# The second state-space unit prepared beside the first one's scan, and loads in another order

## The reference, cut to what matters

```
x = norm(x + state_space(x))     # Mamba-like: convolution, delta = softplus(..), scan over time with 256 x 16 states
x = norm(x + moe(x))             # 16 experts, top 2, and a shared expert
x = norm(x + lstm_attention(x))  # an LSTM of width 20 gives position weights over x
x = norm(x + 4 layers of moe(x)) # 4 experts of width 512, top 2
```

```
h = exp(d_t * A) * h + d_t * b_t * u_t;  y = sum_s(h * c_t)      # then y + D * x_d, times silu(z), projection
c = sigmoid(f) * c + sigmoid(i) * tanh(g);  h = sigmoid(o) * tanh(c)
```

## Time and profile before

| | |
|---|---|
| median of 3 runs | 3143.62 us (3141.18 to 3147.69) |
| the profiled execution, own time | 3143.73 us |
| its span | 3141.7 us |
| mean granted TensorE clock | 0.803 |
| instructions | 30770 |
| HBM read, written | 195.36 MB, 7.34 MB |

### The profile page before, as it was taken

The page is one execution under the profiler, slowest core; times in us unless marked ns, Lnnn a source line. Parts: engine busy times, 40 slices in busy tenths (PEclk is TensorE's granted clock), DMA queues, the critical chain, the costliest instruction groups (busy, mean ns, idle before and its releaser), DMA issues.

```text
span 3141.7 us, 30770 instructions
## 1 busy us (share of the span) xinstructions
PE 2537.0 (81%) x7208; PEld 1271.2 (40%) x7208; DVE 1943.4 (62%) x6569; ACT 1386.7 (44%) x4620; POOL 1062.8 (34%) x913
## 2 busy tenths in 40 slices
PE   4776884479996989789886998788978997889598
PEld 1122443244444444344444443444444444444344
DVE  4857587357775777567766677577766555444422
ACT  3232433435544555445544554445534444444233
POOL 4735257104542445235432455244422001100200
PEclk7587655659996899878996899789978996788699
DMA  3231332003321233113220332122311220111021
GB/s 108 68 84 54 89 99 72 25 13 100 101 66 28 80 96 90 42 46 101 78 71 27 92 97 75 25 73 84 92 33 46 65 64 21 34 64 58 10 81 57
DMA packets 111774, 204.70 MB, mean 65 GB/s; under 512 B 14799, under 2 KB 24422, under 8 KB 111592
## 3 DMA queue, kind: packets, MB, share of 16 engines
q1 hardware_dynamic: 111592, 202.75, 22.1%
HBM read 195.36 MB, written 7.34 MB: 65 GB/s over the span
## 4 chain that ended last, share of the span: by engine, by line
PE 41%; DVE 28%; ACT 14%; issue 7%; POOL 1%; DVEq 0%; POOLq 0%; ACTq 0%
PE p_hid L656 8%; DVE state L1197 7%; PE p_turn L905 7%; PE p_misc L666 4%; ACT cell_t L919 4%; DVE cell L935 3%; DVE add_c L932 3%; PE p_acc L666 3%; DVE weighed L1206 2%; DVE p_turn L929 2%; PE p_misc L354 2%; PE p_gate L465 2%; DVE hist L940 2%; PE p_turn L475 1%; ACT cand L916 1%
## 5 line engine op out<-in xcount | busy, mean ns | idle before, releaser
L905 PEld LDWEIGHTS p_turn<-hist,w_hh 22*128 22x128 f32 x2048 | 371.6, 225 | 1148.2 <-DVE hist L940 1013.9
L905 PE MATMUL p_turn<-hist,w_hh 22*128 22x4 f32 x2048 | 457.3, 291 | 420.2 <-DVE hist L940 402.2
L656 PE MATMUL p_hid<-xhat,w 128*128 128x512 f32 x1024 | 581.8, 652 | 1.1 <-ACT hid L714 0.7
L919 ACT ACTIVATE cell_t<-cell 20x4 f32<-20x4 f32 x1024 | 207.7, 203 | 701.7 <-DVE cell L935 701.7
L1135 POOL TENSOR_TENSOR drive<-du,rows 128x512 f32<-128x512 f32 x256 | 473.4, 1849 | 63.2 <-DVE state L1197 44.9
L929 DVE SCALAR_TENSOR_TENSOR p_turn<-p_turn,cell 20x4 f32<-20x4 f32 x1024 | 170.7, 167 | 500.8 <-ACT p_turn L915 478.9
L714 ACT ACTIVATE hid<-p_hid,b1f 128x512 f32<-128x512 f32 x512 | 351.6, 687 | 243.1 <-PE p_misc L666 151.1
L388 POOL TENSOR_TENSOR n_rstd<-n_var,minus_half 128x4 f32<-128x4 f32 x56 | 62.0, 1108 | 1098.3 <-DVE n_var L376 1098.3
L1197 DVE TENSOR_TENSOR_SCAN state<-decay,drive 128x512 f32<-128x512 f32 x256 | 398.1, 1555 | 25.2 <-POOL drive L1139 15.7
L1154 POOL TENSOR_TENSOR y<-y,weighed 128x512 f32<-128x512 f32 x192 | 242.4, 1262 | 450.5 <-DVE weighed L1206 449.9
L940 DVE SCALAR_TENSOR_TENSOR hist<-p_turn,cell_t 20x4 f32<-20x4 f32 x1024 | 162.7, 159 | 275.6 <-ACT cell_t L919 275.6
(11 more groups left out here) (204 smaller groups left out, 3161.5 us busy)
## 6 DMA issues: line engine op xcount, KB each, us to landing
rows<-rows_dram SPq DMA_DIRECT2D x128, 512.0 KB, 5.0
w<-w_dram SPq DMA_DIRECT2D x128, 256.0 KB, 2.7
w<-in_w2T SPq DMA_DIRECT2D x128, 256.0 KB, 2.7
comb_b<-comb_dram SPq DMA_DIRECT2D x64, 512.0 KB, 4.7
rows<-comb_dram SPq DMA_DIRECT2D x128, 128.0 KB, 2.9
w<-in_w1T SPq DMA_DIRECT2D x16, 256.0 KB, 2.8
w_dram<-w SPq DMA_DIRECT2D x16, 256.0 KB, 2.4
out_xT<-result SPq DMA_DIRECT2D x8, 256.0 KB, 2.5
```

What stands on the lines that cost most here:

```text
L656: nc.tensor.matmul(p_hid[:, v % 2, :], w1[:, v // FB, (v % FB) * P:(v % FB + 1) * P], xhat[:, :], start=True, stop=True).then_inc(g_h, 1)
L905: nc.tensor.matmul(gate_bank(i)[:, :, t:t + 1], w_hh[:, :], before, start=False, stop=False, skip_group_check=True).then_inc(gates_done, 1)
L919: nc.scalar.activation(cell_t[64:64 + PE_, :], cell[32:32 + PE_, :], ACT.Tanh, scale=0.5).then_inc(cell_tanh, 1)
```

## The change

Unit 1 gets storage of its own, in tiles that are not yet in use then, and PSUM banks of its own for its preparation. `first_units` writes the opening anew: unit 0's preparation, then the late loads (on SP), its soft part, its scan with the preparation and ten of the soft slots of unit 1 beside, the leaving of unit 0 with the rest of unit 1's soft part, the scan of unit 1, its leaving, and then unit 2 whole (preparation, soft part, scan, leaving) and the preparation of unit 3. `opening` runs this to the end of unit 0 and then 60 slots of it with layer 0 of chunk 0 beside. `first_period` starts the LSTM there; the rest of the unit schedule goes on beside it, layer 0 of chunk 1 once unit 1 has left, the fold once unit 2 is prepared. `EARLY` is 3, and `scan(u)` in `first_units` passes `True`, so unit 2 is an early unit as well. In a slot the LSTM comes first, then layer 0, the fold, and the units. `mamba_soft_pool` makes both skip terms first and the `kc` products after the drives of the unit before are done. The periods from 1 on keep their order.

```diff
+    as_bt = lambda t: t[:, :, :].rearrange("p j (b t) -> p j b t", b=B)
+    second = dict(xd=comb_b[:, 0:2, :], zs=comb_b[:, 2:4, :], delta=as_bt(xl), du=hid1[:, :, :], y=terms[:, :, :], inc=mw[:, :, :])
+    first = dict(xd=xd[:, :, :], zs=zs[:, :, :], delta=delta[:, :, :, :], du=du[:, :, :], y=y[:, :, :], inc=weighed[:, :, :])
+    of_unit = lambda u: second if u == 1 else first
...
+    def banks(u):
+        if u == 1:
+            return (p_gate[:, :], p_up[:, :]), p_turn[1][:, :], p_turn[0][:, :]
+        return (p_hid[:, 0, :], p_hid[:, 1, :]), p_acc1[:, :], p_misc1[:, :]
...
-        if u:
+        if u > 1:
             pe.wait_ge(ssm_taken, u)
-        if 0 < u <= EARLY:
+        if 1 < u <= EARLY:
             pe.wait_ge(gated, u * NB)
...
         nc.sync.wait_ge(ssm_stored, 16 * (u + 1))
-        for s_ in range(ROWS):
-            load_rows(u, s_)
+        if u != 1:
+            for s_ in range(ROWS):
+                load_rows(u, s_)
...
-    SOFT = 13
+    SOFT, SOFT_A = 14, 10
...
         for j in range(NB):
             pool.wait_ge(delta_done, u * NB + j + 1)
-            nc.gpsimd.tensor_tensor(kc[:, j, :, :], a_neg[:, j, :].rearrange("p (s o) -> p s o", o=1).to_broadcast([P, S, B]),
-                                    delta[:, j, :, 0:1].rearrange("p b o -> p o b").to_broadcast([P, S, B]),
-                                    ALU.mult).then_inc(kc_arg, 1)
-            nc.gpsimd.tensor_scalar(y[:, j, :], xd[:, j, :], d_par[:, j:j + 1], None, ALU.mult).then_inc(y_begun, 1)
+            nc.gpsimd.tensor_scalar(of_unit(u)['y'][:, j, :], of_unit(u)['xd'][:, j, :], d_par[:, j:j + 1], None, ALU.mult)\
+                .then_inc(y_begun, 1)
             yield
             if j == 0:
                 yield
+        if u:
+            pool.wait_ge(drive_done, u * NS)
...
-            if j == 1 and s_ + ROWS - 1 < S and s_:
-                load_rows(u, s_ + ROWS - 1)
+            n = s_ + ROWS - 1
+            if j == 1 and s_ and n < S:
+                load_rows(u, n)
+            if u == 0 and j == 1 and n >= S:
+                load_rows(1, n - S)
+            if u == 1 and k == 0:
+                load_rows(1, ROWS - 1)
...
-    EARLY = 2
+    EARLY = 3
...
+    L0_SLOTS = 60
+    FOLD_SLOTS = 3 * L * E1 + 14
...
+    def first_units(of, seen):
+        get = lambda what, n, u, *a: of[what](u, *a) if what in of else nothing(n)
+        pre = [get("pre", PRE, u) for u in range(EARLY + 1)]
+        soft = [get("soft", SOFT, u) for u in range(EARLY + 1)]
+
+        def scan(u, beside):
+            burst = of["decays"](u) if "decays" in of else nothing(NS)
+            g = get("scan", SCAN, u, True)
+            for k in range(SCAN + 1):
+                for _ in range(6 if k == 0 else 1 if k % 2 == 0 else 0):
+                    next(burst, None)
+                next(g, None)
+                if k:
+                    next(beside, None)
+                yield
...
+        def before(u):
+            yield from run(pre[u], PRE + 1)
+            yield from run(soft[u], SOFT_A)
+
+        yield from run(pre[0], PRE + 1)
+        if "late" in of:
+            of["late"]()
+        yield from run(soft[0], SOFT + 1)
+        yield from scan(0, before(1))
+        yield from both(get("leave", LEAVE, 0, True), soft[1], max(LEAVE, SOFT - SOFT_A) + 1)
+        seen["left"] = 1
+        yield from scan(1, nothing(0))
+        yield from run(get("leave", LEAVE, 1, True), LEAVE + 1)
+        seen["left"] = 2
+        yield from run(pre[2], PRE + 1)
+        seen["pre"] = 2
+        yield from run(soft[2], SOFT + 1)
+        yield from scan(2, nothing(0))
+        yield from run(get("leave", LEAVE, 2, True), LEAVE + 1)
+        yield from run(pre[3], PRE + 1)
+        seen["pre"] = 3
+
+    def opening(of, units, seen):
+        while seen["left"] < 1:
+            next(units)
+        layer0 = of["layer0"](0) if "layer0" in of else nothing(0)
+        for _ in range(L0_SLOTS):
+            next(layer0, None)
+            next(units)
+        for _ in layer0:
+            pass
+
+    def first_period(of, units, seen):
+        lstm = of["lstm"](0) if "lstm" in of else nothing(CH)
+        layer0 = of["layer0"](1) if "layer0" in of else nothing(0)
+        fold = of["fold"]() if "fold" in of else nothing(0)
+        soft, count = (of["soft"](EARLY) if "soft" in of else nothing(SOFT)), 0
+        slot = folds = 0
+        while slot < CH or seen["pre"] < 3:
+            next(lstm, None)
+            if seen["left"] == 2:
+                next(layer0, None)
+            if seen["pre"] >= 2 and folds < FOLD_SLOTS:
+                next(fold, None)
+                folds += 1
+            if seen["pre"] < 3:
+                next(units, None)
+            elif count <= SOFT:
+                next(soft, None)
+                count += 1
+            slot += 1
...
         soft = first_period(of, units, seen)
...
+            def late():
+                for dst, name in ((w_router0[:, :], "w_router0T"), (w_share[:, :], "w_shareT"),
...
+                load_steps(0)
+                load_steps(1)
+                for k in range(E1):
+                    load_raw(k)
```

More of the change, by code:

```diff
@@ new lines, in opening @@
+    def opening(of, units, seen):
[26 more added lines that the diff above has]
+            slot += 1
+        for g in (layer0, fold):
+            for _ in g:
+                pass
+        return [soft, count]
@@ L1419, in period @@
         if u < NCH:
[L1420 removed]
+            scan, leave = get("scan", SCAN, u, False), get("leave", LEAVE, u, False)
         if u + 1 < NCH:
@@ L1423, in period @@
         burst = of["decays"](u) if u < NCH and "decays" in of else nothing(NS)
-        att = att_slots(i - 1) if layer1 else 0
-        ends = att + L * LAYER + 5 if layer1 else 0
-        done = dict(scan=0, leave=0, fold=0, pre=0, soft=0)
-        fold_slots = 3 * L * E1 + 12 + 1
-        slot = 0
+        att = att_slots(i - 1)
+        ends = att + L * LAYER + 5
+        tail = ends - 5
+        done = dict(scan=0, leave=0, pre=0, soft=0)
         def advance(g, what, n):
@@ L1471, in period @@
                     advance(leave, "leave", LEAVE)
-            if u + 1 < NCH and (slot >= tail if i else done["leave"] > LEAVE - 1 and done["fold"] > fold_slots):
+            if u + 1 < NCH and slot >= tail:
                 advance(pre, "pre", PRE)
@@ L1475, in period @@
         for g in (layer1, layer0):
-            for _ in g or ():
+            for _ in g:
                 pass
         return [soft_next, done["soft"]]
-    def opening(of):
-        get = lambda what, u, n, *a: of[what](u, *a) if what in of else nothing(n)
-        def unit(u):
-            burst = of["decays"](u) if "decays" in of else nothing(NS)
-            yield from get("soft", u, SOFT)
-            scan = get("scan", u, SCAN, True)
-            for k in range(SCAN):
-                if k == 0:
-                    for _ in range(6):
-                        next(burst, None)
-                elif k % 2 == 0:
-                    next(burst, None)
-                next(scan)
-                yield
-            next(scan, None)
-            yield from get("leave", u, LEAVE, True)
-            yield from get("pre", u + 1, PRE)
-        for _ in get("pre", 0, PRE):
-            pass
-        for _ in unit(0):
-            pass
-        second = unit(1)
-        layer0 = of["layer0"](0) if "layer0" in of else nothing(0)
-        live = [second, layer0]
-        while live:
-            live = [g for g in live if next(g, live) is not live]
+    HEAVY = 6
+    BURST = {22: 1, 0: 2, 1: 2, 2: 2, 3: 1}
     def whole(of):
-        opening(of)
+        seen = dict(left=0, pre=0)
+        units = first_units(of, seen)
+        opening(of, units, seen)
         if "start" in of:
             of["start"]()
-        soft = [of["soft"](2) if "soft" in of else nothing(SOFT), 0]
-        for i in range(NCH + 1):
+        soft = first_period(of, units, seen)
+        for i in range(1, NCH + 1):
             soft = period(i, of, soft)
@@ L1545, in _ @@
+            whole(dict(late=late, pre=mamba_pre_sp, scan=mamba_scan_sp, leave=mamba_leave_sp, fold=fold_sp, layer0=layer0_sp, layer1=layer1_sp))
             sp.wait_ge(stored, NCH * 16)
```

156 lines of the change are left out of this document (79 added, 77 removed).

## The result

The changed kernel is slower: 3207.65 us median of 4 runs (3201.32 to 3215.18) against 3142.4 us of the kernel before on the same chip (3134.04 to 3147.69), a ratio of 1.021 with a 95% interval of 1.0187 to 1.0233. The forecast was 3200 us.

A forecast was written before the change was run, and what follows sets the result against it. No engine is full; a chain of waits through the LSTM's recurrent matmul bounds the kernel. Opening 286 plus first period 415.4 ends at 701.4 instead of 646.3; with about 1 us more, +56 on 3143.7 gives 3200 us, range 3165 to 3235.

The forecast's parts named there:

- The main term: First period: unit 2's additions on TensorE make the LSTM's next recurrent matmul wait; 34 additions, +87.5 us.
- The forecast slots of 2.3 and 4.6 us: First period, scan alone beside the LSTM: slots would alternate between these lengths, 7 us a scan step against 4.1 before.
- The clock: TensorE in the first period's scan stretch: taken as 1.2 GHz, an addition's price 2.75 us, against 1.85 at 2.4 GHz.
- The case of no change (full clock): Rival, first period: fuller TensorE gets 2.4 GHz, additions cost 30 us less, other work some 25 less; 3145 us, chance 0.12.
- The first period: From the LSTM's first step to the second period: 318.4 + 17.5 - 8 + 87.5 = 415.4 us.
- The opening: Time up to the LSTM's first step: would end at 286 us instead of 327.9, 42 us earlier.
- The fourth row: Scan 0: late loads ahead of this row load on SP's queue delay scan step 6, +8.4 us.
- The work beside scan 0: Opening: unit 1's preparation adds to nearly full VectorE and GpSimd, +12 us, bounds 5 and 25.
- ScalarE table loads that fit into its idle time: Scan 0: ScalarE's part of unit 1's preparation would fit its idle time, busy 21.6 of 94 us; no cost added.
- the 60 slots of layer 0 beside scan 1: Opening's last part, up to the LSTM's start: 27.5, 68, 15.4 and 10.6, sum 121.5 us.
- the last norm: Layer 0 beside scan 1: 8 slots at 3.84 us a scan step, 15.4 us.
- Free additions: Rival, first period: unit 2's additions slip beside the LSTM and relieve GpSimd; period 328 us, time 3111 us, chance 0.16.

The follow-up runs named there:

- e1: Changed kernel with unit 2's sum over states put back on GpSimd: 3122.22 us, ratio 0.9953 to the kernel before.
- e3: Kernel before with only unit 2's early sum added (additions on TensorE in the slot of the multiply): 3219.41 us, ratio 1.0258.
- e2: Changed kernel with unit 2's additions one slot later in TensorE's order, behind the LSTM's next matmul: 3130.51 us, ratio 0.9972.
- e8: Changed kernel with unit 2's sum on GpSimd and unit 1 prepared after unit 0 has left, not beside its scan: 3148.86 us, single run.
- e5: Changed kernel with unit 2's sum on GpSimd and the late loads spread between row loads during scan 0: 3110.58 us, single run.
- e7: Changed kernel with unit 2's sum on GpSimd, late loads spread and unit 1's preparation given one slot in two: 3117.04 us, ratio 0.9947.
- e5b: Timed repeat of e5 (changed kernel, unit 2's sum on GpSimd, late loads spread): 3122.31 us, ratio 0.9944.
- e10: e5b with the additions of units 0 and 1 one slot later in TensorE's order, still 60 slots of layer 0: 3082.63 us, single run.

## Why the prediction was right

- **The main term.** +87.5 us for 34 additions (82 of it for the 32 of unit 2). Measured for the 32: 85.1 us in the changed kernel, 77.8 on the kernel before. Alone beside the LSTM a step costs 7.04 - 4.14 = 2.9 us more, and the forecast had 2.75. The multiply takes 0.92 us and not 0.69 in that place, where GpSimd's drive, begun 0.88 us before it, still runs beside it for 0.38 us. The forecast slots of 2.3 and 4.6 us came as 5.21 and 1.83: the addition falls into the longer slot, the one with the scan, and not into the shorter; the sum of the two is what was forecast. e1 and e3 show the cause by taking it away and by adding it alone, e2 shows that it is the place in the order.
- **The clock.** Taken as 1.2 GHz in the scan stretch, on the ground that it was 0.50 there. It stayed 0.50 with TensorE busy 34.3 of 75 us, although it was 0.59 in the stretch with the experts. The case of no change (full clock) had no part: with the additions in it the stretch stayed at the lower of the two levels. The Trainium skill (TensorE: Matmul & The Clock Gate, What's actually happening) says that the clock goes by how busy the engine has recently been. By that rule, which the prediction set beside its sum, a fuller TensorE could have brought the full clock; here its busy time rose from 13.4 of 47 us to 34.3 of 75 us and the granted clock was 0.50 in both.
- **The first period** was forecast at 415.4 us and took 413.6. Without unit 2's additions it had 415.4 - 82 = 333.4 and took 328.5 (e1).
- **The opening** was forecast to end at 286 us and ended at 295.7, and there terms of the sum were mis-sized, in both directions. Scan 0 began 3.2 us late (45.1 for 41.9, see above). The fourth row cost 11.7 us by step 6 (29.9 - 6 x 3.03, and 11.5 in e8) where +8.4 were put down: the late loads held SP's queue for 36.2 us instead of 33.7, and the row was used 7.4 us after its issue where 6.2 were put down. The work beside scan 0 cost less than its +12: from step 6 to the end pass 84.3 us, and 76.9 in e8 without that work, so 7.4. The words "ScalarE table loads that fit into its idle time" left out its order: it waited for unit 1's convolution with the carry copies behind it. That lay under the wait for the row; where the row's wait is shortened, spacing the preparation gives 3.4 us of scan 0 (e5 and e7). Together scan 0 ended at 159.3 for 157.3, and part of that nearness is luck. The largest miss, 129.6 us for 121.5, is in the 60 slots of layer 0 beside scan 1. It is not in the experts' slots but mostly in the last norm, for which the forecast had four scan steps of 3.84 us, 15.4 in all. They took 21.5:

```profile
258.85 1.22 DVE L1219 TENSOR_TENSOR_SCAN state<-decay,drive 128x512 f32<-128x512 f32 x1
...
280.29 2.31 DVE L1219 TENSOR_TENSOR_SCAN state<-decay,drive 128x512 f32<-128x512 f32 x1
```

  The same four steps take 21.4 us in e5b and 14.5 in e10, so the place of the additions makes them long. The kernel before, from which the pace was taken, has its additions in that place too, but three of them between the last expert's matmul and those of the LSTM's gates (255.79 to 273.04 us, 17.3 us), and the changed one four (260.70 to 281.48 us, 20.8 us). That this one more makes the difference was not run.
- **The overlap** of unit 1 with scan 0 was right in kind: it brings the LSTM's start forward by 21 us (e8, a single run, against e1).
- **Free additions** (0.16) needed under 0.95 us each. e2 comes to 0.4 us a step, but by another order than the change has; what would have made that rival true is one `yield`.

The errors were 10 us too little in the opening and 2 us too much in the first period. That the profiled execution, 3202 us, still came within 2 us of the 3200 is luck: its rest was 4.5 us shorter than before (2490.9 against 2495.4), which no term had. Two slips of the prediction changed nothing: its upper bound of 3235 is more than its named bounds give (3200 + 20 + 6), and scan 1 follows from 157.3 + 7.0 = 164.3, not 164.5.

## What to carry to other kernels

In a schedule in slots, an instruction that waits for a product of its own slot holds back everything behind it on its engine, above all the next turn of a recurrence; put it one slot later, behind the recurrence's instruction, and its time is nearly free. An idle engine is no place for work by its idle share alone: GpSimd at over 90% was harmless here and TensorE at under 30% was not, and the order on the engine decided it. Loads that are moved out of the way stand in the way of the next thing in the same queue, so spread them between the loads that matter.

## What the runs showed that I had not expected

The late loads held SP's queue long without moving much. In the changed kernel, between 48 and 66 us, they moved 2 GB/s (the last column below), and most of the packets of that stretch are of 16 bytes: loads of small pieces, like the router's bias. No run takes these loads away alone; e5 spreads them.

```profile
48.00:56.00 8.00, 7.78 (x13) 3.36 (x14) 5.96 (x5) 0.87 (x1) 7.06 (x6) 0.71 0.05 2
56.00:66.00 10.00, 9.36 (x22) 3.37 (x20) 3.80 (x4) 9.00 (x12) 2.00 (x2) 1.00 0.05 2
```

The fourth row load, issued at 66.03 us behind them, was used at 73.38, 7.4 us later, where the first row load of the earlier trace rows, issued at 46.55, was used at 51.65, 5.1 us later. Also, the same kernel (e5 and e5b) gave 3110.6 and a median of 3122.3 us. The LSTM's start repeats to within 0.5 us over kernels with the same code up to there (295.7, 295.7 and 295.6; 290.4 and 290.9), though the first scan began at 45.1 us in one of them and at 43.1 in the others, so it tells small changes apart better than the time does.
